# One VectorE reduction over two PSUM banks for the row maxima of two heads

## The reference

```python
xn = _group_norm(xf, gn_w, gn_b)
qkv = jnp.einsum('oc,bct->bot', qkv_w, xn) + qkv_b[None, :, None]
qkv = qkv.reshape(b * HEADS, 3 * c // HEADS, T)       # HEADS 8, so 32 channels a head
q, k, v = jnp.split(qkv, 3, axis=1)
weight = jnp.einsum('bct,bcs->bts', q * scale, k * scale)
weight = jax.nn.softmax(weight.astype(jnp.float32), axis=-1)
h = jnp.einsum('bts,bcs->bct', weight, v)
h = jnp.einsum('oc,bct->bot', proj_w, h) + proj_b[None, :, None]
```

```python
sc = jnp.einsum('bqd,bkd->bqk', qm, km) / math.sqrt(qm.shape[-1])
parts.append(jnp.einsum('bqk,bkd->bqd', jax.nn.softmax(sc, axis=-1), vm))
```

## Time and profile before

| | |
|---|---|
| median of 3 runs | 5469.68 us (5468.94 to 5470.98) |
| profiled execution: its own time, span | 5462.21 us, 5460.3 us |
| mean granted TensorE clock | 0.94 of full |
| PE, PEld busy | 4989.7 us (91%), 2248.6 us |
| DVE busy | 2960.1 us (54%) |
| ACT busy | 2558.3 us (47%) |
| POOL busy | 3239.2 us (59%) |

### The profile page before, as it was taken

How to read it: one execution, slowest core, us unless ns; L and a number is a source line. 1 busy time by engine, 2 the same in 40 slices (tenths; PEclk the granted TensorE clock), 3 DMA queues, 4 the chain that set the end, 5 groups by cost and what they waited for, 6 DMA issues and landing times.

```text
span 5460.3 us, 63207 instructions
## 1 busy us (share of the span) xinstructions
PE 4989.7 (91%) x22016; PEld 2248.6 (41%) x22016; DVE 2960.1 (54%) x5256; ACT 2558.3 (47%) x4593; POOL 3239.2 (59%) x1777
## 2 busy tenths in 40 slices
PE   7789999999999999999999998999999999999887
PEld 3235333543335433354334543345333453334434
DVE  5445666256663566526665366634666346662362
ACT  3353545435553355524555245552555525454252
POOL 4474766546674477735767357654667636675463
PEclk8889989999899999999999999999999999899988
DMA  2112111022110211102210112101212012120020
GB/s 85 29 30 59 43 46 39 20 55 54 42 30 20 72 48 33 34 22 64 54 41 19 36 50 55 47 13 44 52 45 53 7 49 61 32 53 10 14 49 12
DMA packets 103608, 221.20 MB, mean 41 GB/s; under 512 B 31104, under 2 KB 33408, under 8 KB 103168
## 3 DMA queue, kind: packets, MB, share of 16 engines
q1 hardware_dynamic: 103296, 217.16, 15.5%
HBM read 56.47 MB, written 8.39 MB: 12 GB/s over the span
## 4 chain that ended last, share of the span: by engine, by line
PE 66%; DVE 11%; issue 9%; POOL 8%; ACT 4%; SPq 1%; DMA 1%; POOLq 0%; DVEq 0%; ACTq 0%
PE bank L518 66%; DVE max_cols L953 6%; POOL probs_added L1181 4%; POOL probs_added L1168 3%; ACT probs L854 2%; DVE act L1108 1%; ACT act L864 1%; DVE dev_squared L1071 1%; DVE stats L1057 1%; POOL act L1202 1%; SPq L1268 0%; DVE sums_turned L975 0%; SPq L1257 0%; DVE sums_turned L983 0%; ACT full_parts L919 0%
## 5 line engine op out<-in xcount | busy, mean ns | idle before, releaser
L953 DVE TENSOR_REDUCE max_cols<-bank 128x1 f32<-128x512 f32 x3456 | 2187.2, 679 | 1642.0 <-PE bank L518 1638.1
L854 ACT ACTIVATE probs<-bank 128x512 f32<-128x512 f32 x3456 | 1928.9, 599 | 2378.1 <-PE bank L518 2248.9
L1181 POOL TENSOR_TENSOR probs_added<-probs_added,probs 128x1024 f32<-128x1024 f32 x768 | 1807.6, 2382 | 131.8 <-ACT probs L854 131.3
L518 PE MATMUL bank<-q_stack,k_stack 97*128 97x512 f32 (+1 forms) x3584 | 1659.9, 520 | 147.2 <-DVE max_cols L953 107.8
L518 PE MATMUL bank<-probs,v_tokens 128*32 128x512 f32 (+1 forms) x7168 | 1392.8, 645 | 41.1 <-ACT probs L854 41.1
L518 PEld LDWEIGHTS bank<-q_stack,k_stack 97*128 97x128 f32 (+1 forms) x3584 | 661.5, 195 | 880.9 <-issue 429.5
L518 PE MATMUL bank<-act,weight_stream 128*128 128x512 f32 x1792 | 941.6, 625 | 31.6 <-ACT probs L854 8.0
L1181 POOL TENSOR_TENSOR probs_added<-probs 128x1024 f32<-128x1024 f32 x192 | 452.5, 2369 | 700.2 <-PE bank L518 673.0
L1168 POOL TENSOR_TENSOR probs_added<-probs 128x512 f32<-128x512 f32 x48 | 61.0, 1270 | 885.7 <-PE bank L518 853.3
L518 PEld LDWEIGHTS bank<-probs,v_tokens 128*32 128x32 f32 (+1 forms) x7168 | 329.6, 123 | 505.6 <-issue 350.8
L518 PE MATMUL bank<-high_parts 32*128 32x512 f32 x3072 | 406.1, 516 | 108.8 <-DVE max_cols L953 59.8
(11 more groups left out here) (84 smaller groups left out, 3390.4 us busy)
## 6 DMA issues: line engine op xcount, KB each, us to landing
k_stack<-high_parts SPq DMA_DIRECT2D x384, 128.0 KB, 2.4
q_stack<-high_parts SPq DMA_DIRECT2D x768, 64.0 KB, 2.0
weight_stream<-stream_dram SPq DMA_DIRECT2D x32, 768.0 KB, 4.3
k_stack<-low_parts SPq DMA_DIRECT2D x192, 128.0 KB, 2.4
q_stack<-low_parts SPq DMA_DIRECT2D x384, 64.0 KB, 2.0
act<-x_dram SPq DMA_DIRECT2D x8, 1024.0 KB, 6.5
act<-pos_dram SPq DMA_DIRECT2D x8, 1024.0 KB, 5.9
weight_stream<-stream_dram SPq DMA_DIRECT2D x16, 512.0 KB, 3.8
```

What stands on the lines that cost most here:

```text
L518: return nc.tensor.matmul(dst, lhsT, rhs, start=start, stop=stop, **kw)
L854: act.activation(PR[:, m % P_RING, j, :], bank[:, :], ACT.Exp, scale=att.scale).then_inc(reading(key), 1)
L953: dve.tensor_reduce(cols[:, kh, j, qt:qt + 1], bank[:, :], AX.X, ALU.max).then_inc(reading(key), 1)
L1181: pool.tensor_tensor(ADD[:, js, :], one, two, ALU.add).then_inc(p_added, 1)
```

## The change

The narrow maxima of two heads are read by one reduction. The 8 banks are declared as 4 pairs that lie side by side, and a quad takes two pairs (`take_pair`), the less recently freed first, which must both be free of held tiles. The matmuls write the same halves as before; only the second of each pair raises `full`, the reduction reads 128 x 2 x 512 and writes two columns, and then raises one `read` for both banks. `emptied` remembers which semaphore and count tell that a bank has been read. In the plan a quad has two "max" events, two units apart, in place of four that are one unit apart; a pair's two banks are given back together at its event. So that whole pairs stay free, a held tile (the values, the sums, a product between attentions) now prefers banks 0 to 3. The wide maxima keep one bank each. No matmul is added or removed.

```diff
--- before.py
+++ after.py
@@ -69,7 +69,8 @@
         self.per = 8 if self.wide else 32
         self.units = self.steps * self.per
         self.adds = 7 if self.wide else 2 * (ADDED - 1)
-        self.maxima = QT * NH * (1 if self.wide else GROUP)
+
+        self.maxima = QT * NH * (1 if self.wide else GROUP // 2)
         self.cols = QT if self.wide else GROUP * QT
 
         self.scale = 1.0 / float(np.sqrt({"m": 4 * P, "3": C}.get(kind, D)))
@@ -151,7 +152,7 @@
     out = []
     for n, (s, quad) in enumerate(pairs):
         out.append((at + n * step, "quad", (s, quad)))
-        out += [(at + n * step + j * apart, "max", (s, GROUP * quad + j)) for j in range(GROUP)]
+        out += [(at + n * step + 2 * j * apart, "max", (s, 2 * quad + j)) for j in range(GROUP // 2)]
     return out
 
 
@@ -316,9 +317,12 @@
     out = []
     if u < att.units:
         for s in range(1, att.steps):
-            first = 2 * (u - att.per * (s - 1)) if att.wide else u - first_quad(s)
-            for p in range(first, first + (2 if att.wide else 1)):
-                if 0 <= p < att.maxima and not (s == 1 and not att.wide and p < GROUP * EARLY_QUADS):
+            if att.wide:
+                first = 2 * (u - att.per * (s - 1))
+                out += [(s, p) for p in range(first, first + 2) if 0 <= p < att.maxima]
+            else:
+                p, r = divmod(u - first_quad(s), 2)
+                if r == 0 and 0 <= p < att.maxima and not (s == 1 and p < 2 * EARLY_QUADS):
                     out.append((s, p))
     return out
 
@@ -424,7 +428,8 @@
         GS = sb("gn_shift", [P, CT])
         PAUSE = sb("pause", [P, 1])
 
-        PS = [ctx.enter_context(nc.psum_tensor(f"bank{i}", [P, HALF], F32)) for i in range(BANKS)]
+        PAIRS = [ctx.enter_context(nc.psum_tensor(f"banks{i}", [P, 2, HALF], F32)) for i in range(BANKS // 2)]
+        PS = [PAIRS[i // 2][:, i % 2, :] for i in range(BANKS)]
 
         def sem(name):
             return ctx.enter_context(nc.semaphore(name))
@@ -520,13 +525,19 @@
             count = {"ws": 0, "h": 0, "gn": 0, "turn": 0}
             uses, fulls, given, held = [0] * BANKS, [0] * BANKS, [0] * BANKS, {}
 
+            emptied = [(i, 0) for i in range(BANKS)]
+
             def take(key, hold=False, says_full=True):
 
-                bank = min((i for i in range(BANKS) if i not in held.values()), key=lambda i: (given[i], i))
+
+                bank = min((i for i in range(BANKS) if i not in held.values()),
+                           key=lambda i: (hold and i >= BANKS // 2, given[i], i))
                 tiles[key] = bank, uses[bank], fulls[bank]
-                if uses[bank]:
-                    pe.wait_ge(read[bank], uses[bank])
+                i, n = emptied[bank]
+                if n:
+                    pe.wait_ge(read[i], n)
                 uses[bank] += 1
+                emptied[bank] = bank, uses[bank]
                 fulls[bank] += says_full
                 count["turn"] += 1
                 given[bank] = count["turn"]
@@ -534,9 +545,28 @@
                     held[key] = bank
                 return PS[bank]
 
+            def take_pair(key):
+
+                busy = [i // 2 for i in held.values()]
+                pair = min((i for i in range(BANKS // 2) if i not in busy),
+                           key=lambda i: (max(given[2 * i], given[2 * i + 1]), i))
+                a, b = 2 * pair, 2 * pair + 1
+                tiles[key] = a, uses[a], fulls[a]
+                for i, n in {emptied[a], emptied[b]}:
+                    if n:
+                        pe.wait_ge(read[i], n)
+                uses[a] += 1
+                fulls[a] += 1
+                emptied[a] = emptied[b] = a, uses[a]
+                count["turn"] += 1
+                held[key], held[key, 1] = a, b
+                return PS[a], PS[b]
+
             def give(key):
                 count["turn"] += 1
                 given[held.pop(key)] = count["turn"]
+                if (key, 1) in held:
+                    given[held.pop((key, 1))] = count["turn"]
 
             def stream_w(i):
                 return WS[:, 512 * i:512 * i + 512]
@@ -646,12 +676,15 @@
                     until_read(pe, ("q", att.index, (g, s % NH)))
                 qt, kh = divmod(n, NH)
                 q0 = s % NH * HALF + qt * P
-                keys = [("max", att.index, s, GROUP * n + j) for j in range(GROUP)]
-                banks = [take(key, True) for key in keys]
-                for j, key in enumerate(keys):
+                keys = [("max", att.index, s, 2 * n + j) for j in range(GROUP // 2)]
+                banks = [bank for key in keys for bank in take_pair(key)]
+                for j, bank in enumerate(banks):
                     r = slice(D * j, D * j + D)
-                    mm(banks[j][:, :], HIS[r, g, 0, q0:q0 + P], HIS[r, g, 1, half(kh)], True, True,
-                       tile_position=(D * j, 0)).then_inc(filling(key), 1)
+                    ins = mm(bank, HIS[r, g, 0, q0:q0 + P], HIS[r, g, 1, half(kh)], True, True,
+                             tile_position=(D * j, 0))
+
+                    if j % 2:
+                        ins.then_inc(filling(keys[j // 2]), 1)
 
             def columns(att, s):
                 key = ("cols", att.index, s)
@@ -944,13 +977,18 @@
                     qt, kh = divmod(p, NH)
                     j = 0
                 else:
-                    qt, kh, j = p // (NH * GROUP), p // GROUP % NH, p % GROUP
+                    qt, kh, j = p // GROUP, p // 2 % NH, 2 * (p % 2)
                 cols = MC[:, turn % 2, :, :, :]
                 if p == 0 and turn >= 2:
                     dve.wait_ge(nm_ready, turn - 1)
                 key = ("max", att.index, s, p)
                 bank = until_full(dve, key)
-                dve.tensor_reduce(cols[:, kh, j, qt:qt + 1], bank[:, :], AX.X, ALU.max).then_inc(reading(key), 1)
+                if att.wide:
+                    ins = dve.tensor_reduce(cols[:, kh, j, qt:qt + 1], bank[:, :], AX.X, ALU.max)
+                else:
+                    both = PAIRS[tiles[key][0] // 2]
+                    ins = dve.tensor_reduce(cols[:, kh, j:j + 2, qt], both[:, :, :], AX.X, ALU.max)
+                ins.then_inc(reading(key), 1)
                 if p == att.maxima - 1:
                     until_read(dve, key)
                     both = cols[:, :, 0, :].rearrange("p k q -> p q k") if att.wide else \
```

## The result

The changed kernel takes 5711.59 us, the median of 4 runs (5710.36 to 5716.56); the kernel before, beside it on the same chip, 5469.31 (4 runs). The ratio is 1.0447 [1.0429, 1.0465]: 242 us slower. The forecast of 5598 had the direction, but the time lies above its range, 5475 to 5690. The profiled execution has a span of 5708.6 us, against 5460.3 before.

What follows compares the result with a forecast made beforehand. The kernel was taken as bound by TensorE's list. New waits of 256 us less 85 gone make 171, times 0.75 is 128; 5462.2 + 128 = 5590, and 7.5 us to the median gives 5598, range 5475 to 5690.

Steps and rivals of the forecast that it cites:

- The reduction over two banks: VectorE's joined reading of a pair: 1212 ns, one every 1.13 us in a row, saving 103 us of busy time.
- The mechanism at a score: TensorE's second score behind a quad: the first bank comes free 0.53 us later, so its 0.35 us wait grows by that.
- the latency of one reduction, with VectorE nowhere behind: TensorE's wait at a quad's second score: for the first reduction alone, 0.68 us, after VectorE sat idle 2.67 us.
- The other edits cost nothing that I can see: Rest of the change: plan events are no instructions, semaphore waits are fewer, no DMA moves; put at no cost.
- Scores and quads: TensorE's waits for banks at narrow scores and quads: 256 us added less 85 gone, 171, counted as 128 us.
- The factor 0.75: Share of the 171 us counted, from TensorE's 66% and its issue's 9% of the chain; gives 128 us.
- The mean tile: Quads waiting for a pair that holds the group norm's mean tile: 14 by 31 us, one starting 2.4 us later.
- Throughput (1): Rival at VectorE: its throughput counts, so the kernel gets some 60 us faster, 5410; chance 0.13 together with the early-free pair.
- A pair free at 0.7 us (2): Rival: the reduction overlaps its two banks, freeing both at 0.7 us; 5300 to 5420 us; chance 0.13 together with throughput.
- Absorbed (3): Rival: added waits fall where TensorE would wait anyway; 5470, or up to 5530 us; chance 0.10 for 5481 to 5530.
- The clock (4): Rival at TensorE: more gaps lower the mean clock to 0.92, some 5680 us; chance 0.12 for above 5650.
- The semaphores: Two raises a quad instead of four: VectorE might start 0.05 us earlier at each, up to 40 us less, 5558.

Runs made afterwards that it cites:

- e6: Kernel before, own banks and single reductions; heads 0 and 1, and 2 and 3, read back to back, both banks free after the second; 5610.04 us, ratio 1.0260.
- e3: Changed kernel with each pair read by two reductions, still released once after the second; 5756.64 us, 1.0549 of the kernel before.
- e1: Changed kernel with its choice of banks, but each bank filled, read by its own reduction and released alone; 5641.69 us, 1.0336 of the kernel before.
- e4: Kernel before, single reductions and banks, but held tiles other than a quad's prefer banks 0 to 3; 5647.50 us, ratio 1.0346.
- e11: Changed kernel, but a held tile takes the bank given back longest unless fewer than two whole pairs would remain; 5630.40 us, 1.0311 of the kernel before.
- e12: Kernel before with each quad's matmuls moved ahead of the values' matmuls of the same unit; 5597.20 us, ratio 1.0252.
- e14: Kernel before, single reductions, with banks released in twos and all held tiles preferring banks 0 to 3; 5834.15 us, ratio 1.0672.
- e7: Kernel before, own banks; where two of a quad's are neighbours, heads 2 and 3 go there and one reduction reads both; 5458.52 us, ratio 0.9984.

## Why the prediction was wrong

**The reduction over two banks: right.** 1217 ns against 1212 forecast, and two in a row take 2.36 us, so the second starts 1.14 us behind the first. VectorE's saving was 81 us for 103.

**The mechanism at a score: right.** 0.89 us at the quad of the earlier trace rows. e6 and e3 show that the release in twos costs 142 us in the old banks and 116 in the new ones. The 128 us of the prediction are not borne out by this: they were for the joined reading with its shorter release, and that costs 61 us against e1 (1.0447 - 1.0336).

What was read too widely is the earlier trace rows itself. Of the 188.0 us that TensorE waits for maxima before, only 41.9 (106 waits) end with the first reduction that VectorE makes after it was idle, sorted as in e3; in the changed kernel it is 173.9 (285) of 363.5. So "the latency of one reduction, with VectorE nowhere behind" was the smaller part of the waits of before, and is three quarters of those that the change added.

**"The other edits cost nothing that I can see": this step failed.** What it put at nothing was the largest term. The preference for banks 0 to 3 costs 189 us on the old kernel (e4), and the whole choice of banks 183 without a late release (e1). The walk through the lists took every narrow score and every quad, but no product and no norm tile as a *taker* of a bank; they stood in it only as tiles in a quad's way. At these the idle time grew by 97 us (products) and by 16 at the group norm's `mean_var` tiles. The row that would have led there was in reach, the 31.6 us of the products before: so little because that kernel gives a tile the bank longest free, which the edit takes away.

**Scores and quads: right in kind, too large.** The term of 171 us, 128 after the factor 0.75, is 35 + 35 = 70 us of idle time in the changed kernel. The factor was a guess from the chain's shares. The products' waits now stand ahead of scores, and waits at scores ahead of quads: between e1 and the changed kernel 99 of 108 us only changed place. How much of the difference to 128 this explains was not measured. That this term was too large hides a part of what was left out: without it the time would lie still further above the range. That is luck. The chance of 0.12 for more than 5650 us was given to the clock, which did not fall, and so does not cover this result.

**The mean tile: right in kind, a quarter of the size.** In the changed kernel the quad of the earlier trace rows is held up:

```profile
2831.61 2.36 DVE L990 TENSOR_REDUCE max_cols<-banks 128x2 f32<-128x1024 f32 x2 [0.43 <-PE banks L523]
...
2832.89 0.38 PE L523 MATMUL banks<-mean_var,weights 128*128 128x2 f32 x2 [0.75 <-DVE max_cols L990]
...
2833.89 1.93 PE L523 MATMUL banks<-probs,v_tokens 128*32 128x512 f32 x8
...
2836.24 0.14 DVE L1110 TENSOR_SCALAR group_mean<-banks 128x2 f32<-128x2 f32 x1
...
2836.53 0.80 PE L523 MATMUL banks<-high_parts 32*128 32x512 f32 x4 [0.71 <-DVE group_mean L1110]
```

and before:

```profile
2712.34 2.48 DVE L953 TENSOR_REDUCE max_cols<-bank 128x1 f32<-128x512 f32 x4
...
2712.46 0.35 PE L518 MATMUL bank<-mean_var,weights 128*128 128x2 f32 x2
...
2714.12 1.07 PE L518 MATMUL bank<-probs,v_tokens 128*32 128x512 f32 x8
```

TensorE stands 0.71 us, not 2.4. From the start of these reductions it came to the quad after 4.21 us (2835.82), before after 2.78 (2715.12), while the norm's tile was read after 4.77 us, before after 5.10. It came later for two reasons. The norm's own matmul had already stood 0.75 us for the first pair, as it now takes a bank that the quad ahead had filled, and started 1.28 us after the reductions for 0.12. And the eight matmuls of the values took 1.93 us where they took 1.07. The stretch of those matmuls (columns as in the earlier trace rows) shows the clock at 0.50, its lower level of 1.2 GHz:

```profile
2833.90:2836.50 2.60, 1.92 (x9) 0.19 (x8) 2.45 (x5) 0.83 (x2) 2.40 (x2) 0.50 0.01 3
```

In the trace of before the same eight ran at 1.00. The forecast had kept the pace and the order of the old trace. Over the whole kernel 11 quads wait for `group_mean`, 0.9 us at the most and 8.3 us in sum, where 14 with 31 us were forecast. The other 30.3 of its 38.6 us are the seven waits before `act,weights`, which the prediction did not have. The preference alone does not bring them (e4), the release in twos on the old banks brings 19.2 us of them (e6), and e11 has none.

**The rivals.** Throughput (1) is part of the 45 to 56 us of the joined reading (e3), where the rival had some 60; it is outweighed. Its own test was that most of the 188 us stem from a reduction that started late. 146.1 of them do have other work of VectorE just ahead, which speaks for it, and yet the kernel became slower: the test did not weigh what the new waits cost. A pair free at 0.7 us (2) is out, by the 1217 ns. Absorbed (3): in part, as scores' waits took the place of quads' (e1 against the changed kernel). The clock (4) is not the cause in the changed kernel (0.939 for 0.940, busy time up 28 of 248 us), though it is a part of e4, e12 and e14.

**The semaphores.** Where VectorE was idle, its reduction started 0.534 us after a quad's first matmul before, and 0.543 after (medians), with half the raises. So the 0.05 us by which it might have started earlier did not come. The Trainium skill ("TensorE: Matmul & The Clock Gate", the per-tile semaphore tail) says that the raises of concurrent tiles come one after the other, and so how long the last of them takes. That was not tested here, since VectorE waited before for the first of four raises, and waits now for the first of two, that of the second matmul: e1, with four raises, has 0.534 too, and e3, with two, 0.543.

**What stays open.** The causes don't add in one way only: release in twos 142 or 116 us by the order in which it is put in; and for the banks 183 us (e1, the whole choice) and 189 (e4, the preference alone) don't say what whole pairs cost or give apart from it. Open are also the cost of the new order of VectorE's list by itself, and whether e7's 0.16%, which goes with the clock, is a gain to rely on.

## What to carry to other kernels

In a ring of PSUM banks that is nearly full, when a bank comes free counts for more than how fast the reader gets through all of them (116 against 56 us): join reads at most where nobody waits for the first bank soon. Even that gave little here (heads 2 and 3: -10 us, with no less waiting; heads 0 and 1: +44 us). When a rule of allocation changes, take every kind of tile through the new list, above all those that did not wait before; "no instruction added" is no price. If a layout needs neighbours kept free, ask for that condition itself (e11) and not for a fixed half, which costs 74 us more here.

## What the runs showed of the hardware

One reduction reads across the border of two banks at the same pace as within one: 1217 ns for 1024 elements, 679 for 512, so 1.05 ns an element. Instructions in a row overlap by the same 0.08 us at both sizes (1217 to a pitch of 1140, 679 to 600 ns). The mean granted clock moved between 0.930 and 0.950 among kernels with the same matmuls, and not by the sum of the gaps: e14 and e3 are both idle for 734 us, at 0.930 and 0.942, and TensorE is busy 5097.2 and 5008.9 us. What in the pattern of the gaps decides it was not tested. The kernel before by itself, in the 42 executions beside the experiments, moved between 0.938 and 0.944, and the lower the clock, the longer the time: some 4 us for each 0.001, an estimate from a line fitted through them (correlation -0.83).
